# Perceiver block with experts on one core: two low halves of the first expert tile's weights, made by GpSimd at the end of self-attention or by VectorE behind it

## The reference

```python
# x (64, 32, 512) and ctx (64, 257, 256), all float32
x = x + cross_attention(layernorm(x), ctx)      # 16 heads of 32
x = x + self_attention(layernorm(x))            # 16 heads, RoPE, latent keys and values
x = x + experts(layernorm(x))                   # 8 experts, top 2

# experts, for xf = (2048, 512) tokens
gate_logits = xf @ Wr
w, idx = top_k(gate_logits, 2);  w = softmax(w)
comb = sum(w[:, :, None] * one_hot(idx, 8), axis=1)
h = einsum('nc,ech->neh', xf, W1);  g = einsum('nc,ech->neh', xf, W3)      # hidden size 768
y = einsum('neh,ehc->nec', silu(h) * g, W2)
out = einsum('nec,ne->nc', y, comb)
```

## Time and profile before

| | us |
|---|---|
| median of 3 runs | 1495.09 |
| lowest and highest | 1493.82 and 1500.4 |
| span of the profiled execution | 1492.9 |
| TensorE busy | 1434.5 |
| VectorE busy | 1088.6 |
| ScalarE busy | 807.5 |
| GpSimd busy | 543.6 |

### The profile page before, as it was taken

The page is one execution under the profiler, slowest core; times in us unless marked ns, Lnnn a source line. Parts: engine busy times, 40 slices in busy tenths (PEclk is TensorE's granted clock), DMA queues, the critical chain, the costliest instruction groups (busy, mean ns, idle before and its releaser), DMA issues. The chain is left out here.

```text
span 1492.9 us, 39481 instructions
## 1 busy us (share of the span) xinstructions
PE 1434.5 (96%) x14944; PEld 1281.3 (86%) x14944; DVE 1088.6 (73%) x1945; ACT 807.5 (54%) x1525; POOL 543.6 (36%) x810
## 2 busy tenths in 40 slices
PE   7999999999999999998999998799999999999998
PEld 6888888988888888887778786698999999999997
DVE  3676777767777677776667686797887878787785
ACT  4666666666666666654434434345555545555452
POOL 1222222221222222224866876453333333333232
PEclk9999999999999999999999999899999999999999
DMA  6301101000001100100011014179877878787871
GB/s 239 125 28 31 30 22 29 29 22 29 22 28 28 29 28 23 30 9 1 31 38 38 32 38 155 57 220 314 281 263 247 286 253 267 262 279 238 292 256 44
DMA packets 130734, 174.11 MB, mean 117 GB/s; under 512 B 16953, under 2 KB 89337, under 8 KB 130626
## 3 DMA queue, kind: packets, MB, share of 16 engines
q1 hardware_dynamic: 120242, 145.56, 30.1%
q0 software_dynamic: 10384, 27.05, 5.0%
HBM read 157.18 MB, written 19.06 MB: 118 GB/s over the span
## 5 line engine op out<-in xcount | busy, mean ns | idle before, releaser
L2229 DVE TENSOR_TENSOR split<-raw,split 128x1024 fp32r<-128x1024 f32 x204 | 242.3, 1220 | 7.2 <-ACT split L2169 6.0
L52 PE MATMUL bank<-split_xT,split 128*128 128x256 f32 x768 | 216.5, 282 | 0.4 <-DVE split L2229 0.2
L54 PE MATMUL bank<-split_xT,split 128*128 128x256 f32 x768 | 215.4, 281 | 0.0
L53 PE MATMUL bank<-split_xT,split 128*128 128x256 f32 x768 | 215.4, 280 | 0.0
L2169 ACT CAST split<-raw 128x1024 fp32r<-128x1024 f32 x202 | 203.2, 1048 | 6.9 <-DMA raw<-in_L_ffn_W_dram 3.2
L596 ACT ACTIVATE Pr<-xa_s,nmax 128x257 f32<-128x257 f32 x256 | 118.7, 473 | 124.9 <-DVE nmax L696 124.8
L2189 ACT ACTIVATE sl<-bank 128x256 f32<-128x256 f32 x115 | 44.2, 384 | 240.8 <-PE bank L54 223.5
L52 PE MATMUL xa_s<-split,split 128*128 128x258 f32 x512 | 150.5, 294 | 1.9 <-DVE split L628 1.9
L52 PEld LDWEIGHTS bank<-split_xT,split 128*128 128x128 f32 x768 | 144.9, 189 | 7.0 <-issue 2.8
L53 PEld LDWEIGHTS bank<-split_xT,split 128*128 128x128 f32 x768 | 145.0, 189 | 3.1
L53 PE MATMUL xa_s<-split,split 128*128 128x258 f32 x512 | 145.6, 284 | 0.0
(11 more groups left out here) (317 smaller groups left out, 3915.1 us busy)
## 6 DMA issues: line engine op xcount, KB each, us to landing
raw<-in_L_ffn_W_dram SPq DMA_DIRECT2D x207, 512.0 KB
raw<-in_ctx_dram SPq DMA_DIRECT2D x64, 256.0 KB, 2.6
out_dram<-x_res SPq DMA_DIRECT2D x16, 256.0 KB
xs<-xn SPq DMA_DIRECT2D x16, 256.0 KB
x_res<-in_x_dram SPq DMA_DIRECT2D x1, 3584.0 KB, 18.7
VL<-v_last_rows SPq DMA_DIRECT2D x128, 2.0 KB, 1.5
raw_o<-in_L_xattn_Wo_dram SPq DMA_DIRECT2D x1, 1024.0 KB, 6.4
raw_q<-in_L_xattn_Wq_dram SPq DMA_DIRECT2D x1, 1024.0 KB, 9.5
```

Source lines behind the costliest of these rows:

```text
L52: pe.matmul(out, lh, rh, start=start, stop=False)
L53: pe.matmul(out, ll, rh, start=False, stop=False)
L54: return pe.matmul(out, lh, rl, start=False, stop=stop)
L2229: vW.done(dve.tensor_tensor(lo, raw, hi.bitcast(F32), ALU.subtract), f"p{c}{q}")
```

## The change

The low halves of the pieces (1, 0) and (1, 1) of the first tile are made by GpSimd, in self-attention's block, behind its last send and ahead of its last wait. VectorE no longer makes them in the first tile; its next low half, piece (1, 2), now waits until the counter `vW` has passed p11.

```diff
--- before.py
+++ after.py
@@ -1613,6 +1613,15 @@
                 power(vN2, gN2, aN2, b, mvb, rstdb, shiftb)
                 for j in range(n_early + 2, late_from):
                     send(j)
+
+                def first_low(q):
+                    raw, hi, lo = first_tile.part(held, 1, q)
+                    flow.aW.wait(pool, 0, f"p1{q}")
+                    flow.vW.wait(pool, 0, f"p1{q - 1}" if q else "p02")
+                    flow.vW.done(pool.tensor_tensor(lo, raw, hi.bitcast(F32), ALU.subtract), f"p1{q}")
+
+                first_low(0)
+                first_low(1)
                 pool.wait_ge(sent_early, 32 * n_early)
 
 
@@ -2226,6 +2235,8 @@
                 def split(t, pos, c, q):
                     raw, hi, lo = part(c, q)
                     aW.wait(dve, index(t, pos), f"p{c}{q}")
+                    if isinstance(t, int) and (t, pos, c, q) == (0, 0, 1, 2):
+                        vW.wait(dve, 0, "p11")
                     vW.done(dve.tensor_tensor(lo, raw, hi.bitcast(F32), ALU.subtract), f"p{c}{q}")
 
                 def splits(t, pos, place, last):
@@ -2289,9 +2300,6 @@
                                 f"{pos}a{j}")
                         if j == NH - 1 and not last:
                             x_lo(*following(t, pos))
-                        if first and j == 0:
-                            for c, q in in_attention:
-                                split(t, pos, c, q)
                         splits(t, pos, j, last)
                         if first:
                             for n in fills.get(j, []):
```

## The result

The changed kernel takes 1499.2 us in the median of 22 runs, the kernel before 1495.65 in the median of 22: a ratio of 1.0019 with a 95% interval of 1.0011 to 1.0027. That is a loss of 2.8 us (1.6 to 4.0) by the ratio and of 3.6 by the medians, smaller than 0.5% and clear of noise. The profiled execution has a span of 1497.6 us, that of before 1492.9.

The account below looks back on a forecast made before the run. VectorE's routing chain ahead of the block's end, and TensorE behind it, were taken to bound the kernel. Chain +4.1, removal 0, clock 0 added to the median 1495.09 gave 1499.2 us, range 1495.0 to 1503.0.

Parts of the forecast that it names:

- What bounds the kernel: Around the block's end: VectorE's routing chain ahead of it sets the end, TensorE behind it; a microsecond added to the chain counts fully.
- The removal: First expert tile: VectorE's two subtractions, 2.35 us together, dropped; TensorE did not wait for them, so worth 0, at most 0.3.
- The width: GpSimd's subtraction of 1024 columns, behind its last send: 2361 ns each, with the fixed 197 ns paid once.
- What the two do to each other: Routing chain: a small two-SBUF-input VectorE instruction waits for a GpSimd tensor_tensor already running, ending 0.05 us behind it.
- Rival 1: Routing chain: VectorE's small instructions slip between parts of GpSimd's long one; loss 0 to 0.5 us, 1495.1 to 1495.6; chance 0.10.
- rival 3: Behind the last send: GpSimd's halves take 4.3 us each, costing +7.9, 1503.0 us, slower by over 0.5%; chance 0.06.
- The sum: Whole kernel: chain +4.1, removal 0, clock 0, together +4.1 us, giving 1499.2 us.
- the chain's term: Routing chain ahead of the block's end: two held instructions, one for each GpSimd half, lengthen it by about 4.1 us.
- the first hold: Routing chain: L1394 at 961.47 held by the half running 961.18 to 963.54, ending at 963.59; +1.95 us.
- The signs that I had named: Trace: halves of 2.4 us, two held instructions, L1394 first, chain end about 971, TensorE idle 4 longer, VectorE waiting at j = 2.
- one sign that I had named as speaking against the forecast: First expert tile: the forecast is wrong if this tile ends sooner against the block's end; no size given.
- The clock: TensorE's restart behind the idle gap at 1.2 GHz: same cost as before, taken as 0, bounds -2.8 and +2.8 us.

Follow-up runs that it names:

- add_only: Kernel before, with GpSimd also making the two low halves behind its last send while VectorE still makes them; ratio 1.0025, 3.7 us more than before.
- four_halves: Changed kernel, with GpSimd making each of the two low halves twice, four instructions instead of two; ratio 1.0049 to the kernel before, 7.3 us more.
- remove_only: Changed kernel, with GpSimd's two subtractions one column wide instead of 1024, so neither engine spends time on them; ratio 1.0014 to the kernel before.
- memsets: Kernel before, with five GpSimd memsets of 128x1024 over the low halves' places behind the last send; ratio 1.0001.
- earlier: Changed kernel, with GpSimd's two halves moved ahead of the routing chain, behind the sends of tiles 12 and 13; ratio 1.0017 to the kernel before.
- pieces: Changed kernel, with each half cut into four GpSimd pieces of 128x256, eight instructions in all; ratio 1.0020 to the kernel before, 3.0 us more.
- gap: Changed kernel, with one GpSimd addition of 128x1 between the last send and the first half; ratio 1.0030 to the kernel before, 4.5 us more.

## Why the prediction was right

**What bounds the kernel: right.** Work that holds the chain makes it longer, and the kernel with it (add_only: 4.3 and 3.7 us, four_halves: 7.2 and 7.3); VectorE's work taken away behind the block's end brought no gain that can be measured.

**The removal: right, from one profile that was kind to it.** I put it at 0, at most 0.3. VectorE waits for the silu at j = 2, as said, and remove_only gives no gain. I had also said that at j = 3 VectorE would be where it was; it now even waits 0.38 us there. But the gapless first tile that I built on isn't in every execution. In the second profile of the kernel before TensorE had its full clock back sooner, VectorE had no pause in the tile, and TensorE waited for it at the tile's end. That is the first row here, the second is the changed kernel's:

```profile
990.55 0.47 PE L52 MATMUL bank<-split,a_hi 128*128 128x512 f32 x1 [1.05 <-DVE a_lo L2288]
991.66 0.47 PE L52 MATMUL bank<-split,a_hi 128*128 128x512 f32 x1 [0.20 <-DVE a_lo L2299]
```

With the two subtractions in VectorE's program this wait is 0.31 and 1.05 us in the two profiles of before, 0.30 in add_only and 0.88 in memsets; in all three of the changed kernel it is 0.19 to 0.20. So in some executions the removal can take up to 0.85 us off the first tile. Whether that reaches the end of the kernel isn't shown.

**The width: right.** I took 2 x 1279 - 197 = 2361 ns; the row by line of the changed kernel gives 2339, 2362 and 2384 ns (least, median, most). The last nanosecond is chance, since the two halves differ by 45:

```profile
L1621 POOL TENSOR_TENSOR split<-raw,split x2: 2339/2362/2384, 958.7 to 961.2; 128x1024 fp32r<-128x1024 f32 x2
```

**What the two do to each other: right.** One small instruction is held for each half and ends 0.03 to 0.04 us behind it. Rival 1, that short instructions slip through, falls with the same rows; rival 3 too, since no half took over 2.4 us.

**The sum: the mechanism right, the chain's term too small.** I had 4.1 us, the trace has 4.98. The term that was mis-sized is the start of the first hold: I began it at GpSimd's row and placed it so that 0.3 us of the chain ran beside the first half. The hold began about 0.5 us ahead of the row, since the half was queued behind the send, and the first instruction it met was held for 2.93 us. With a small instruction in between the chain loses 4.06, close to the number that I had worked out.

**The signs that I had named.** The length of the halves, the two held instructions and the wait for the silu came as named. Others didn't. L1397 was held first, not L1394, and the chain ended at 968.27, not at 971, since it began 3.7 us earlier. TensorE's idle time ahead of a_lo, which I had 4 us longer, is 4.51 us in place of 4.76. I had looked for the waiting in the wrong place: both holds lie ahead of the block's last two products on TensorE, and it waits ahead of those. Before, then after:

```profile
963.15 0.40 PE L1082 MATMUL bank<-both,below 128*128 128x24 f32 x2 [1.04 <-DVE both L1402]
...
964.45 0.62 PE L1082 MATMUL bank<-both,below 128*128 128x24 f32 x2 [3.27 <-DVE both L1402]
```

And one sign that I had named as speaking against the forecast did show: the first tile ends sooner against the block's end, 991.66 - 968.27 = 23.39 us behind it, where before it was 990.98 - 966.98 = 24.00. The shorter tile makes it, and the clock most of that.

**The clock.** TensorE restarted at the lower level as before (a granted clock of 0.50 in 972 to 974 in both profiles). Full clock came back about 4.5 us behind the restart in place of 5.6, and the first tile was a little shorter: 990.98 - 968.71 = 22.27 us before and 991.66 - 970.01 = 21.65 after, up to TensorE's next wait for a_lo. That is within the bounds that I gave the clock. The longer chain has no part in it that the runs show: in the second profile of before it took 3.1 us and the tile 21.91, in the other two of the changed kernel about 4 us and 21.58 and 21.46.

**The net.** A chain 4.98 us longer, with nothing gained behind, should be 5 us; measured are 2.8 (1.6 to 4.0) by the ratio and 3.6 by the medians. So 1 to 3 us are missing. The kernels of this study, by how much longer the chain of their profile is and how much slower they are than before (us, with the 95% interval):

| kernel | chain longer by | slower by |
|---|---|---|
| memsets | +0.35 | 0.1 (-2.5 to 2.7) |
| earlier | 0 | 2.5 (0.1 to 4.9) |
| remove_only | +0.10 | 2.1 (-0.1 to 4.3) |
| pieces | +3.29 | 3.0 (0.1 to 5.8) |
| gap | +4.06 | 4.5 (2.1 to 6.9) |
| add_only | +4.30 | 3.7 (1.3 to 6.0) |
| changed | +4.98 | 2.8 (1.6 to 4.0) |
| four_halves | +7.24 | 7.3 (4.6 to 10.2) |

Where the kernel before only gets work added (memsets, add_only) the time follows the chain, and in four_halves and gap too. The changed kernel lies below its chain, and earlier and remove_only, whose chains aren't held, lie some 2 us above theirs. What these two share with the changed kernel, and add_only and memsets don't have, is the missing work in the first tile and the moved counter steps. That this brings a small loss of its own is a rival that no run separates; pieces, gap and four_halves, which have it too, lie within 0.5 us of their chains. It would leave even more missing in the changed kernel. What could make up for it are some 0.6 us of the shorter first tile and the earlier start of the chain in all three of its profiles (3.0 to 3.9 us), which has the right sign but wasn't isolated. It stays open.

That the predicted 1499.2 us is the measured median is luck. The chain's term was 0.9 too small, something unexplained of 1 to 3 us goes the other way, and the median of before in 22 runs is 0.56 above the one I started from.

## What to carry to other kernels

Before handing work to an engine that seems idle, look at what the other engine does in that time and from where it reads. Beside a GpSimd tensor_tensor that was there first, VectorE's next instruction with two SBUF inputs is held to GpSimd's end (3.10 and 2.23 us in place of 0.17), so a long GpSimd instruction beside a chain of short dependent ones costs nearly its own length, whatever it was meant to save. VectorE's reductions, with one input, passed beside the halves in 0.17 us, and in earlier an addition of 128x512 with one input in PSUM kept its 0.69 us; a tensor_scalar, though it has one input, was held in memsets. A stretch of the first two kinds, or one in which VectorE waits, is the place to try. And first ask who waits for the work that is moved: here hardly anyone did.

## What the runs showed of the hardware that I had not expected

A GpSimd instruction queued straight behind an indirect DMA holds VectorE before its own row begins: in all three profiles of the changed kernel L1397, begun 0.31 or 0.32 us behind the send's start, took 3.10 or 3.11 us. It should have been over 0.5 us before the row of the half begins. A GpSimd addition of one column between the two did away with it. GpSimd's price for a tensor_tensor with two SBUF inputs is 732 ns at 256 columns, 1279 at 512 and 2362 at 1024, that is 2.1 ns a column and 0.19 us once. And five memsets of 1024 columns, 5.03 us in all, leave two-input instructions at 0.17 us and hold only a tensor_scalar of 2 columns, for 0.53 us.
